# Row maxima of an attention kernel: turned as four squares and sent in two transfers, with the first products 12 steps ahead

## The reference, cut to what matters

```python
att = jnp.einsum('bhnd,bhmd->bhnm', q, k) * scale
att = jax.nn.softmax(att, axis=-1)
out = jnp.einsum('bhnm,bhmd->bhnd', att, v)
...
x = _layernorm(x + _L0_attn_ref(x, ...), axis=-1)
x = _layernorm(x + _L0_ffn_ref(x, ...), axis=-1)
```

## Time and profile before

| what | value |
|---|---|
| median of 3 runs | 3693.47 us (3684.49 to 3722.55) |
| the profiled execution, its own time | 3681.82 us |
| its span in the trace | 3680.0 us |
| granted TensorE clock, mean | 0.995 |
| busy: TensorE, VectorE, ScalarE, GpSimd | 99%, 90%, 72%, 23% |
| attention stage | 258.5 us to about 2788 us |
| transfers of maxima | 1024, 1.0 KB each |
| VectorE transposes | 128, 211 ns each |

### The profile page before, as it was taken

The page is one execution under the profiler, slowest core; times in us unless marked ns, Lnnn a source line. Parts: engine busy times, 40 slices in busy tenths (PEclk is TensorE's granted clock), DMA queues, the critical chain, the costliest instruction groups (busy, mean ns, idle before and its releaser), DMA issues. The chain is left out here.

```text
span 3680.0 us, 83726 instructions
## 1 busy us (share of the span) xinstructions
PE 3642.5 (99%) x31004; PEld 2094.3 (57%) x31004; DVE 3317.8 (90%) x4142; ACT 2657.4 (72%) x4971; POOL 843.7 (23%) x553
## 2 busy tenths in 40 slices
PE   9999999999999999999999999999998999999998
PEld 5664444444444444444444444444446999999998
DVE  9879999999999999999999999999994877777785
ACT  3428888888888888888888888888884343343433
POOL 6530300000000000000000000000005778787775
PEclk9999999999999999999999999999999999999999
DMA  8993125115113311611421241151111222221220
GB/s 295 348 238 69 60 42 72 37 34 75 42 38 52 61 38 30 83 38 35 64 53 38 42 72 38 33 77 42 38 57 60 90 82 78 68 91 68 86 73 29
DMA packets 327909, 272.80 MB, mean 74 GB/s; under 512 B 170929, under 2 KB 237489, under 8 KB 327602
## 3 DMA queue, kind: packets, MB, share of 16 engines
q1 hardware_dynamic: 326482, 264.38, 29.1%
q0 software_dynamic: 1120, 4.19, 0.4%
HBM read 157.30 MB, written 110.10 MB: 73 GB/s over the span
## 5 line engine op out<-in xcount | busy, mean ns | idle before, releaser
L780 DVE TENSOR_REDUCE half_max<-first_ps 128x2 f32<-128x1024 f32 x2032 | 2381.7, 1218 | 59.7 <-PE first_ps L606 6.9
L746 ACT ACTIVATE probs<-score_ps 128x512 f32<-128x512 f32 x4096 | 2169.1, 598 | 326.2 <-PE score_ps L620 277.7
L633 PE MATMUL pv_ps<-probs,v_s 128*32 128x320 f32 (+1 forms) x16384 | 1205.7, 389 | 0.0
L620 PE MATMUL score_ps<-q_s,k_s 49*128 49x512 f32 x4096 | 1165.0, 435 | 0.1
L606 PE MATMUL first_ps<-k_s,q_s 48*128 48x512 f32 x4064 | 1051.3, 442 | 3.3 <-PEq L189 3.0
L620 PEld LDWEIGHTS score_ps<-q_s,k_s 49*128 49x128 f32 x4096 | 579.7, 185 | 457.4 <-ACT probs L746 423.1
L633 PEld LDWEIGHTS pv_ps<-probs,v_s 128*32 128x32 f32 x16384 | 358.2, 108 | 583.2 <-issue 485.3
L606 PEld LDWEIGHTS first_ps<-k_s,q_s 48*128 48x128 f32 x4064 | 434.0, 185 | 336.1 <-issue 209.2
L896 POOL TENSOR_TENSOR num<-num,rden 128x1024 f32<-128x1024 f32 x2 | 4.7, 2368 | 2356.6 <-DMA rden<-rden_d 2356.6
L1071 ACT ACTIVATE act_f<-fc_ps,b 128x512 f32<-128x512 f32 x256 | 174.7, 683 | 456.5 <-PE fc_ps L1024 452.8
L1148 DVE CAST a_hi<-act_f 128x512 fp32r<-128x512 f32 x256 | 260.6, 1018 | 136.9 <-ACT act_f L1071 136.7
(11 more groups left out here) (115 smaller groups left out, 2556.4 us busy)
## 6 DMA issues: line engine op xcount, KB each, us to landing
q_s<-q_hi_d SPq DMA_DIRECT2D x512, 64.0 KB, 2.1
x_t<-x_c_in SPq DMA_DIRECT2D x32, 512.0 KB, 5.3
q_hi_d<-q_hi SPq DMA_DIRECT2D x32, 512.0 KB, 4.2
q_lo_d<-q_lo SPq DMA_DIRECT2D x32, 512.0 KB, 4.6
k_s<-k_hi_d SPq DMA_DIRECT2D x128, 128.0 KB, 4.2
q_s<-q_lo_d SPq DMA_DIRECT2D x256, 64.0 KB, 2.1
q_s<-max_row SPq DMA_DIRECT2D x1024, 1.0 KB
o_d<-o_sb SPq DMA_DIRECT2D x64, 256.0 KB, 2.1
```

The source lines that it names most:

```text
L620: pe.matmul(bank(k)[:, :], k_s[g][at, a, t * P:(t + 1) * P], q_s[g][at, a, :], start=True, stop=True).then_inc(scored, 1)
L633: last = pe.matmul(pv_ps[h * VC:(h + 1) * VC, queries], v_s[g][:, t, h, :], probs[k % DEEP][:, h, queries], start=t == 0 and part == 0, st ...
L746: nc.scalar.activation(probs[k % DEEP][:, u, :], bank(4 * k + u)[:, :], ACT.Exp).then_inc(exped, 1)
L780: dve.reduce_max(half_max[g % 2][:, :, a * TT + t, keys], first_ps[keys][:, :, :], AX.X)\
```

## The change

`max_row` becomes a tile of 32 partitions x 128 in place of 128 x 32. `rows` turns the four squares of `neg_max` with four instructions of 32 x 32, all of whose results lie on the same 32 partitions, side by side; only the last of them signals. A row of 128 queries is then in one piece, and `load_max` needs two transfers of 8 x 128 values (one for each half of the partitions) where it had eight. `LEAD` goes from 14 to 12. With that, `TURN` goes from step 1 to step 3 of a group, and two parts fewer are done ahead of the loop and two more inside it.

```diff
-LEAD = 14
+LEAD = 12
...
-        max_row = [sb(f"max_row{i}", [P, SQ]) for i in two]
+        max_row = [sb(f"max_row{i}", [SQ, P]) for i in two]
...
-        QL, KVL, ML, OS = 6 * 16, 7 * 16, 2 * (P // SQ) * 16, 16
+        QL, KVL, ML, OS = 6 * 16, 7 * 16, 2 * 16, 16
...
-                    for k in range(P // SQ):
-                        square = max_row[g % 2][k * SQ + h * 2 * TT:k * SQ + (h + 1) * 2 * TT, :]
-                        sp.dma_start(row[:, :, k * SQ:(k + 1) * SQ].bitcast(F32), square).then_inc(m_loaded[g], 16)
+                    sp.dma_start(row.bitcast(F32), max_row[g % 2][h * 2 * TT:(h + 1) * 2 * TT, :]).then_inc(m_loaded[g], 16)
...
-                dve.transpose(max_row[g % 2][:, :], neg_max[g % 2][:, :].bitcast(F32)).then_inc(row_up, 1)
+                for k in range(P // SQ):
+                    square = slice(k * SQ, (k + 1) * SQ)
+                    done = dve.transpose(max_row[g % 2][:, square], neg_max[g % 2][square, :].bitcast(F32))
+                done.then_inc(row_up, 1)
```

## The result

The changed kernel takes 3757.99 us (median of 4 runs, 3754.62 to 3798.12), the kernel before 3690.23 (median of 4). The ratio is 1.0184, with a 95% interval of 1.0132 to 1.0236: slower, clear of the noise. The forecast was 3737, in a range of 3702 to 3768. The profiled executions are 3759.5 and 3681.8 us, 77.7 apart, where the sum had said 44.2.

What follows compares the result with a forecast made beforehand. TensorE's order of work was taken to set the pace, with VectorE's slack at the turn used up. 50.6 - 2.5 - 4.5 + 0.6 = +44.2 us on 3693.5 gave 3737, range 3702 to 3768.

Steps and rivals of the forecast that it cites:

- The place: At the turn in each group: slack is used up, so added VectorE work shows on TensorE in full, 0.405 us a group.
- I take 0.135: Four turns in each group: each added turn costs 0.135 us (bounds 0.06 to 0.211), +50.6 us over 125 groups.
- turns do not overlap each other: Rival, the four turns: 0.211 us each, 79 - 6.4 = +73 us, 3766; chance 0.06.
- The transfers: Two row transfers in place of eight: off the path; four fifths of the issue time go.
- Nothing but those waits: Two transfers in place of eight: the saved issue time gains only the 7 score waits, 2.5 us together.
- The start: Ahead of the loop: two parts fewer, four maxima of 1.13 us, -4.5 us; clock effect put at 0, 6 us either way.
- The end: Behind the loop: reciprocals, SyncE's store and GpSimd's product come later, ending at 2769.1 against 2768.54 wanted, +0.6 us.
- The row too late: Rival, scores' wait for the row with LEAD 12: 0.5 us beyond its 1.4 us spare would give 3800; chance 0.03.
- The cheaper turn: Rival, chain of four maxima behind the turn: at 0.095 us a turn the sum is 29 us, 3723; chance 0.28.
- the delay that is not seen: Rival, TensorE's wait at the turn: something else would impose it anyway; only -6.4 us remains, 3687; chance 0.08.
- the queue's term: Transfer queue with LEAD 12: two steps more to load, so the scores' 7 waits for the row go, -2.5 us.

Runs made afterwards that it cites:

- e6: The kernel before with LEAD 16 and the turn four maxima behind the negation, eight transfers, one whole turn; 1.0017 of the kernel before.
- e2: The kernel before with three more whole turns of the 128 x 32 tile, into spare tiles, ahead of the real one; 3750.06 us (one run).
- e3: The kernel before with LEAD 12 and nothing else (one turn, eight transfers); 4877.74 us (one run).
- e4: The kernel before with six more short instructions (whole turn, two copies, three square turns) ahead of its turn; 3811.65 us (one run).
- e8: The kernel before with three more turns of a 32 x 32 square, all from band 0 to band 0, ahead of its turn; 3723.52 us (one run).
- e11: The kernel before with the first group's eight transfers of maxima moved to ScalarE's queue and nothing else; 1.0005 of the kernel before.
- e9: The kernel before with three more square turns from bands 1, 2 and 3 into band 0, ahead of its turn; 3764.25 us (one run).

## Why the prediction was right, and where it was off

The direction and the mechanism held. *The place*: what VectorE gets more at the turn shows on TensorE in full. Measured, negation to maximum went from 0.36 to 1.00 us, +0.64, and the period from 19.58 to 20.20, +0.62; the table above shows the same for six kernels. e6 shows the other side: with the delays apart, the loads' waits for VectorE fall from 36.5 to 11.9 us in 1000, and three periods of four lie 0.1 us under the old mean (19.43 to 19.46).

*The term that was mis-sized* is the price of a turn, "I take 0.135". It measured 0.213. The row was the right instruction with the wrong neighbour: a maximum that reads the other memory is free to overlap, a turn that reads the next band is not. With 0.213 the sum is 125 x 0.64 = 80, and 80 + 0.6 - 2.5 - 4.5 = 73.6, against 77.7. That outcome stood as a rival, "turns do not overlap each other", with 3766 and a chance of 0.06, and it is what happened, though its name is too wide: whole turns do overlap (e2). The changed band was in the diff, and the bounds did hold it. That the number fell in the range is owed to this: the range reached up to a rival with a chance of 0.06, while the forecast itself was 33 us short between the profiled executions.

*The transfers*: right off the path, but the -2.5 us was too much. Two issues take 1.38 us, and the scores' waits for the row fell from 2.0 to 1.0 us. Those 2.5 us were waits of the weight loader: the view in the earlier trace rows names no product that waited for the row, and the longest period from 618 to 2691 us is 19.79, 0.23 over the mean. "Nothing but those waits" was on the other side too little said: e3 shows that the two transfers carry the shorter lead.

*The start*: -3.7 for -4.5; from 274 to 288 us the granted clock is 0.64 in place of 0.51, a difference that was put at 0. *The end*: a wait of 1.00 us for +0.6. *The row too late*: it did not happen.

*The cheaper turn* and *the delay that is not seen* are both refuted by the changed kernel's timeline. The gain that the change could have had, the start's 3.7 us, is a twentieth of what it pays in the loop.

What stays open: why TensorE sometimes keeps the lower clock for 67 to 110 us. In the three traces that have one such stretch (e2, e4, e6) it begins at or behind a wait of 7.34, 2.56 and 1.18 us, but waits about as long stand in e2 (1.24) and e8 (6.56) without one. The five long runs of e11 left no trace. Of the 4 us between 73.6 and 77.7, the queue's term holds up to 2.5, the start 0.8 and the rest of the program 1.0.

## What to carry to other kernels

Price an added instruction by the pair that it forms with its forerunner, not alone: on VectorE a turn of 32 columns cost 0.09 us behind another on the same band of partitions and 0.21 on another band. Work for an engine that has time to spare on average still has a place; put it where the engine's buffers aren't already being waited for, or spread it: the four turns in place of one cost 78 us together and 14 spread. When a lead is changed, look at every queue that feeds the first steps: with a lead of 16, moving eight transfers off one of them brought the long runs from nine of 12 to one.

## What the runs showed of the hardware

A VectorE instruction that reads from or writes to another band of 32 partitions than the one ahead starts only when that one has ended. Turns of a square with changed bands start 0.213 us apart (e9 and the changed kernel), on the same band they add 0.09 each (e8).

A wait of TensorE can cost more than its length. In e3, about 2 us of waiting in seven groups of ten went with a mean granted clock of 0.66 to 0.71 in the stage, and the kernel went from 3691 to 4878 us. How long the lower clock lasts doesn't follow the length of the wait: one of 1.18 us in e6 was followed by 110 us at 1.2 GHz with TensorE busy throughout, one of 1.24 us in e2 by none. One of 7.34 us in e2 had 78 us at 1.2 GHz with it, one of 6.56 us in e8 less than 20.
